# A large fused kernel on one core: the up weights of both expert stages made stationary, copied for each tile, with scaled result copies taken in turns

## Chip, cores and metric

The kernel runs on one core of one Trainium2 chip. The metric is the device time of one execution in microseconds (us), lower is better. A core has the engines TensorE (PE), VectorE (DVE), ScalarE (ACT), GpSimd (POOL) and SyncE (SP); each has an instruction queue of its own, and they meet through semaphores.

## What is computed

Two layers over a sequence of S = 4096 tokens of width D = 256, all float32. Layer 0 is x + SSD(xn) + MoE0(xn), layer 1 is x + attention(xn) + MoE1(xn), where xn is the layer norm of x. The change touches the two expert parts only:

```python
def _swiglu(x, w1, w3, w2):
    return jax.nn.silu(x @ w1.T) * (x @ w3.T) @ w2.T
# MoE0: 16 experts of width 128, 4 chosen for each token (grouped top-k of sigmoid scores)
# MoE1: 8 experts of width 512, 2 chosen for each token (softmax of the two top scores):
h1 = jnp.einsum('bsd,efd->bsef', x, W1)
h2 = jnp.einsum('bsd,efd->bsef', x, W2)
hidden = jax.nn.silu(h1) * h2
expert_out = jnp.einsum('bsef,edf->bsed', hidden, W3)
return jnp.einsum('bse,bsed->bsd', gating, expert_out)
```

The expert's result for a token is scaled by the token's gate weight and summed over its chosen experts.

## The kernel before

The program runs in stages: norm and routing of layer 0, the SSD stage (to about 1380 us), the first expert stage ("e0_", 1381 to 1631 us), the bridge (sum of the expert rows, layer norm, attention, routing of layer 1), and the second expert stage ("e1_", from 1910 us to the end). Both expert stages are the function expert_phase (from line 1218), with other sizes.

Routing has sorted the (token, expert) pairs into tiles of 128 rows, each tile of one expert: NT0 = 144 tiles in the first stage with f = 128, NT1 = 72 in the second with f = 512. A table etab in SBUF gives each tile's expert. All up weights (wup, 2f columns an expert) and down weights (wdown) of the stage lie in SBUF once SP has loaded them, expert after expert.

For each tile the kernel gathers its 128 token rows (xg), turns them on PE with two transposes (x_ps), copies them to SBUF (xgT, DVE), multiplies by the up weights (u_ps), takes silu of the first half (sil, ACT), multiplies sil, gate and the second half (hid, DVE), turns hid on PE with f/128 transposes (h_ps), copies that to SBUF (hidT, ACT), multiplies by the down weights (d_ps), copies the result (y, DVE), and POOL scatters the rows by an indirect DMA. In the first stage y goes to rows of its own; in the second it is added into the output in memory, one tile after another, each add waiting for the one before.

In the up matmul of before the stationary operand is xgT (128x128 of it, tokens as columns) and the moving one is the weights, read straight from wup at an address that depends on the expert: passes of 2f = 256 columns in the first stage, of 512 columns in two PSUM banks (UB = 2) in the second. u_ps has tokens as rows, and so hid has to be turned before the down matmul.

The order on every engine is the helper pipeline(nt, 3, step), which calls step once for each tile and three times more; in step s an engine works on tile s, s-1 (a), s-2 (b) and s-3 (c or d) as written out. On PE: x transposes of s (line 1394), up of s-1 (1405), the register load of the expert number of s (1386), hid transposes of s-2 (1416), down of s-3 (1424). On ACT: the DMA of a row tile eight tiles ahead (1331, first stage only), silu of s-1 (1343), hidT of s-2 (1348). On DVE: xgT of s (1359), in the first stage a piece of the Join work (1491 and 1497: 64 operations of 128x256 that sum x, SSD and shared rows, spread over tiles 54 to 139), hid of s-1 (1367), y of s-3 (1374). On POOL, first stage: target rows of s (1291), six bias adds of 128x1024 (1478, at tiles 50, 61, ... 105, each after a DMA of shared rows that SP issues in line 1455), scatter of s-3 (1308). On POOL, second stage: gather of s (1286), add of s-7 (1300). The rings: u_ps 2, sil, hid and hidT 2, y six tiles in the first stage and four in the second, d_ps two banks in the first stage and one in the second. SP loads the weights in lines 1213 and 1214.

Of the kernel before, what the change touches and what calls it, by code (L numbers as in the profile page):

```python
# [12 lines left out]
P = 128  # L13
# [1204 lines left out]
def expert_phase(nc, sem, tag, k, rows, lists, by_slot, etab, wup, wdown, e_n, f, nt, y_dram, load, s_first=None, beside=None):  # L1218
# [8 lines left out]
    with ctx:  # L1227
# [4 lines left out]
        AHEAD = 8  # L1232
# [4 lines left out]
        hid = sb("hid", [P, 2, f])  # L1237
        hidT = sb("hidT", [P, 2, f])
# [7 lines left out]
        h_ps = ps("h_ps")  # L1246
        d_ps = [ps("d0"), ps("d1")] if UB == 1 else [ps("d0")] * 2
        RD = 2 if UB == 1 else 1
# [3 lines left out]
        s_xt, s_xk, s_up, s_sil, s_hid, s_ht, s_hk, s_dn, s_yk = (sem(tag + n) for n in (  # L1252
            "x_turned", "x_kept", "up_done", "silu_done", "hidden", "hidden_turned", "hidden_kept",
            "down_done", "y_kept"))
        with nc.Block() as block:
# [25 lines left out]
            def _(pool):  # L1281
# [12 lines left out]
                def add_rows(n):  # L1294
                    pool.wait_ge(s_yk, n + 1)
# [8 lines left out]
                def scatter(n):  # L1304
                    pool.wait_ge(s_yk, n + 1)
# [21 lines left out]
            def _(act):  # L1327
                def next_rows(n):
                    act.wait_ge(s_hid, n - XR + 1)
                    act.wait_ge(s_target, n - XR + 1)  # L1330
                    act.dma_start(xg[:, n % XR, :], by_slot[n * P:(n + 1) * P, :]).then_inc(s_xg[n % XR], 16)
# [3 lines left out]

                def step(s):
                    if sorted_rows and XR <= s.n + AHEAD < nt:
                        next_rows(s.n + AHEAD)
# [5 lines left out]
                    b = s.back(2)  # L1344
                    if b.inside(nt):
                        reached(act, s_ht, b)
                        reached(act, s_dn, b, 2)
                        nc.scalar.activation(hidT[:, b.slot(2), :], h_ps[:, 0:f], ACT.Copy).then_inc(s_hk, 1)
# [3 lines left out]
            def _(dve):  # L1352
                v = nc.vector

                def step(s):
                    if s.inside(nt):
                        reached(dve, s_xt, s)
                        reached(dve, s_up, s, 2)
                        v.tensor_copy(xgT[:, s.slot(2)].rearrange("p c t -> p (c t)"), x_ps[:, 0:D]).then_inc(s_xk, 1)  # L1359
                    if beside:  # L1360
                        beside.tile(dve, s.n)
                    a = s.back(1)
                    if a.inside(nt):
                        reached(dve, s_sil, a)
                        reached(dve, s_ht, a, 2)
                        second = u_ps[a.slot(2)][UB - 1][:, f * (2 - UB):f * (3 - UB)] if UB == 1 else u_ps[a.slot(2)][1][:, 0:f]
# [13 lines left out]
            def _(pe):  # L1380
                held = {}

                def expert(s):

                    if s.n not in held:
                        held[s.n] = pe.value_load(etab[0:1, ds(s.n, 1)], min_val=0, max_val=e_n - 1)
                    return held[s.n]

                def step(s):
# [19 lines left out]
                    if s.inside(nt):  # L1409
# [746 lines left out]
```

## Time and profile before

| | |
|---|---|
| Median of three runs | 2352.23 us (2347.92 to 2357.65) |
| The profiled execution, its own time | 2354.6 us |
| Its span in the profile | 2352.9 us |
| Mean granted TensorE clock | 0.973 of full speed |
| PE busy, of the span | 2170.1 us, 92% |
| PE weight loads | 1588.1 us, 67% |
| DVE, ACT, POOL busy | 68%, 50%, 61% |
| DMA | 329 MB, 140 GB/s on average |

A page of the profile shows one execution. Busy times of an engine exclude register, branch, semaphore and DMA-issuing instructions. PE and PEld are TensorE's matmuls and its weight loads, which overlap. The ends of matmuls are modelled: a matmul record lasts longer than the distance to the next one. L1405 is line 1405 of the kernel. PEclk is the clock that was granted to TensorE, as a share of full speed.

### The profile page before, as it was taken

The page shows a single profiled execution, that of the slowest core. Times are in us where ns is not written, and L with a number is a line of the kernel's source. Part 1 is how long each engine was busy: PE and PEld are TensorE (multiplying, and loading weights), DVE is VectorE, ACT ScalarE, POOL GpSimd, SP SyncE. Part 2 cuts the span into 40 slices and gives each one's busy share as a digit, 9 for nine tenths or more (in the row PEclk, how much of TensorE's full clock was granted, in tenths as well). Part 3 has the DMA queues.
Part 4 walks back from the last instruction along what each step waited for, and adds up shares of the span by engine and source line. Part 5 has one row for each costly group of instructions (what it writes and reads, how often), then busy time and mean ns, then how long its engine had stood idle before and what let it go on. Part 6 is the DMA issues. An engine that isn't in the chain of part 4 may idle for free. (4 is left out here: it accounts for less than half of the span.)

```text
span 2352.9 us, 40732 instructions
## 1 busy us (share of the span) xinstructions
PE 2170.1 (92%) x12292; PEld 1588.1 (67%) x12292; DVE 1601.6 (68%) x3508; ACT 1186.1 (50%) x2671; POOL 1423.7 (61%) x1272
## 2 busy tenths in 40 slices
PE   4878999999999999999999989998698779999997
PEld 2446777777777777777777768786344656666665
DVE  5777888888888888888888856775878632222222
ACT  2456777777777777777777732222132431111111
POOL 1325777777777777777777757886635014444442
PEclk9998999999999999999999999999799889999999
DMA  9854444454454544555544548874520055222221
GB/s 322 320 134 129 140 140 140 138 157 137 146 152 143 144 135 147 146 153 144 149 140 135 144 129 250 271 249 158 208 95 1 1 203 150 45 45 43 44 45 19
DMA packets 193828, 329.02 MB, mean 140 GB/s; under 512 B 49236, under 2 KB 135509, under 8 KB 193365
## 3 DMA queue, kind: packets, MB, share of 16 engines
q1 hardware_dynamic: 137220, 232.12, 33.2%
q0 software_dynamic: 26880, 53.64, 8.8%
q10 hardware_dynamic: 29520, 40.66, 5.4%
q8 instruction: 110, 1.80, 0.3%
q14 instruction: 98, 0.79, 0.1%
HBM read 240.46 MB, written 86.79 MB: 139 GB/s over the span
## 5 line engine op out<-in xcount | busy, mean ns | idle before, releaser
L1014 DVE SCALAR_TENSOR_TENSOR m_cv<-m_hp,conv,m_cv 128x256 f32<-128x256 f32 x864 | 416.7, 482 | 112.1 <-ACT m_cv L913 90.9
L1405 PE MATMUL e_u<-wup,e_xgT 128*128 x1152 | 413.1, 492 | 0.5 <-DMA wdn<-in_w 0.5
L1343 ACT ACTIVATE e_sil<-e_u 128x128 f32<-128x128 f32 (+1 forms) x216 | 82.9, 384 | 525.2 <-PE e_u L1405 525.2
L840 POOL TENSOR_TENSOR m_er<-m_er,m_cT 128x1024 f32<-128x1024 f32 x128 | 301.7, 2357 | 45.8 <-DVE m_ar L1021 45.8
L951 ACT ACTIVATE m_ar<-m_ar,m_ta 128x128 f32<-128x128 f32 x1024 | 318.8, 390 | 0.8
L1102 PE MATMUL m_hp<-xnT,wpj 128*128 128x259 f32 x1152 | 304.7, 387 | 7.8 <-PEq L145 4.5
L1405 PEld LDWEIGHTS e_u<-wup,e_xgT 128*128 128x128 f32 x1152 | 205.2, 193 | 113.9 <-issue 105.9
L1110 PE MATMUL m_gp<-xnT,wpj 128*128 128x256 f32 x1024 | 268.7, 384 | 11.2 <-ACT m_gT L931 11.2
L1102 PEld LDWEIGHTS m_hp<-xnT,wpj 128*128 128x128 f32 x1152 | 214.1, 192 | 68.7 <-issue 27.4
L1300 POOL DMA_INDIRECT out<-e_y,target x72 | 113.0, 1569 | 229.2 <-DVE e_y L1374 199.3
L847 POOL TENSOR_TENSOR m_hdd<-m_hdt,m_tb 128x512 f32<-128x512 f32 x128 | 130.8, 1041 | 194.1 <-DVE m_hdt L1029 194.1
L1161 PE MATMUL m_out<-wo,m_gT 128*128 128x256 f32 x1024 | 242.9, 380 | 0.0
L931 ACT ACTIVATE m_gT<-m_gp,bias 128x256 f32<-128x256 f32 x256 | 121.1, 473 | 232.6 <-PE m_gp L1110 232.5
L1367 DVE SCALAR_TENSOR_TENSOR e_hid<-e_sil,gate,e_u 128x512 f32<-128x512 f32 x72 | 53.8, 747 | 255.2 <-ACT e_sil L1343 255.2
L1424 PE MATMUL e_d<-wdn,e_hidT 128*128 x864 | 224.3, 382 | 1.1 <-DVE e_y L1374 1.1
L1161 PEld LDWEIGHTS m_out<-wo,m_gT 128*128 128x128 f32 x1024 | 193.0, 190 | 47.7 <-issue 23.9
L1110 PEld LDWEIGHTS m_gp<-xnT,wpj 128*128 128x128 f32 x1024 | 178.6, 191 | 35.8 <-ACT m_gT L931 19.1
L881 POOL DMA_INDIRECT rows_by_slot<-m_xrow,posi x128 | 172.1, 1344 | 32.7 <-issue 28.2
L913 ACT ACTIVATE m_cv<-m_hp,m_bsum,conv 128x256 f32<-128x256 f32 x288 | 160.1, 556 | 56.9 <-PE m_hp L1102 55.3
L1308 POOL DMA_INDIRECT y_rows<-e_y,e_target x144 | 145.0, 1007 | 47.9 <-DVE e_y L1374 35.3
L1424 PEld LDWEIGHTS e_d<-wdn,e_hidT 128*128 128x128 f32 x864 | 147.3, 190 | 24.0 <-issue 2.1
L1047 DVE SCALAR_TENSOR_TENSOR m_y<-m_hT,dcol,m_yt 128x128 f32<-128x128 f32 x512 | 143.1, 342 | 23.7 <-PE m_yt L1150 23.7
(313 smaller groups left out, 3965.3 us busy)
## 6 DMA issues: line engine op xcount, KB each, us to landing
m_ar<-acum_rows_dram SPq DMA_DIRECT2D x512, 128.0 KB, 3.9
m_er<-eacum_rows_dram SPq DMA_DIRECT2D x128, 512.0 KB, 4.3
rows_by_slot<-blank_rows ACTq DMA_DIRECT2D x1, 18576.0 KB, 82.1
e_xg<-rows_by_slot ACTq DMA_DIRECT2D x132, 129.0 KB, 3.4
m_xrow<-xn_rows SPq DMA_DIRECT2D x32, 512.0 KB, 4.9
b_work<-y_rows SPq DMA_DIRECT2D x16, 1024.0 KB, 7.1
wup<-in_w SPq DMA_DIRECT2D x8, 1024.0 KB, 5.5
wpj<-in_w_proj SPq DMA_DIRECT2D x1, 4352.0 KB, 24.0
```

Source lines behind the costliest of these rows:

```text
L840: g.tensor_tensor(er[:, t], er[:, t], middle(cT[:, t * P:(t + 1) * P], HQ), ALU.mult).then_inc(scaled.sem, 1)
L881: pool.indirect_dma_start(by_slot, bass.IndirectOffsetOnAxis(posi[:, i * TB + t, r:r + 1], 0), xrow[:, t, r, :], None).then_inc(s_scat[t], 16)
L913: a(cv[:, n % 6, :], hp[n % 2][:, OLD:PW], ACT.Identity, bias=bsum[:, c:c + 1], scale=conv[:, c, OLD:TAPS]).then_inc(heva.sem, 1)
L951: ins = a(row, row, ACT.Exp, bias=ta[:, t, q * HQ + h:q * HQ + h + 1])
L1014: v_.scalar_tensor_tensor(o, hp[n % 2][:, j:j + BLK], conv[:, c, j:j + 1], o, ALU.mult, ALU.add).then_inc(tapped.sem, 1)
L1047: ins = v_.scalar_tensor_tensor(y1[:, cols], hT[:, conv_of(cc), t * P:(t + 1) * P], d_col[:, cc:cc + 1], yt[s % 2][:, cols], ALU.mult, ALU ...
L1102: ins = mm(hp[n % 2][:, 0:PW], w_proj[:, kd, col:col + P], xpad[:, kd, ds(i * BLK, PW)], start=kd == 0, stop=kd == KD - 1)
L1110: ins = mm(gp[:, 0:BLK], w_proj[:, kd, cc * P:(cc + 1) * P], xpad[:, kd, ds(i * BLK + OLD, BLK)], start=kd == 0, stop=kd == KD - 1)
L1161: ins = mm(out_ps[:, t * D:(t + 1) * D], gT[:, q % 2 * CQ + c, t * P:(t + 1) * P], w_out[:, cc, :], start=s == 0 and c == 0, stop=cc == CH ...
L1308: pool.indirect_dma_start(y_dram, bass.IndirectOffsetOnAxis(row_of(n), 0), y[:, n % YR, :], None).then_inc(s_y[n % YR], 16)
L1405: ins = nc.tensor.matmul(u_ps[a.slot(2)][b][:, 0:width], xgT[:, a.slot(2), c, :], wup[:, c, ds(e * (2 * f) + b * width, width)], start=c = ...
L1424: ins = nc.tensor.matmul(d_ps[d.slot(2)][:, 0:D], hidT[:, d.slot(2), c * P:(c + 1) * P], wdown[:, ds(e * (FC * D) + c * D, D)], start=c == ...
```

## The change

Both stages: the up weights become the stationary operand. Since the expert is only known at run time, ACT (and DVE for half of it in the second stage, halves = not sorted_rows) copies the tile's expert weights from wup into a ring of two, fixed, at fixed addresses; in the second stage that ring lies in the columns of xnT, which are free by then. The moving operand is xgT, 128 columns. The products come out with the hidden units as rows, as the down matmul wants them, so the hid transposes, h_ps and hidT go. With tokens as columns the gate can't be applied to hid any more, so it scales the result copy y: even tiles on ACT, odd tiles on DVE, each with a PSUM bank and a semaphore of its own. PE, ACT (and DVE in the second stage) each load the expert number into a register, a tile ahead. hid gets a ring of three, the row tiles are fetched seven ahead in place of eight.

```diff
-        AHEAD = 8
+        AHEAD = 7
-        hid = sb("hid", [P, 2, f])
-        hidT = sb("hidT", [P, 2, f])
+        hid = sb("hid", [P, 3, f])
+        halves = not sorted_rows
+        fixed = (xnT[:, :, 0:KD * 2 * f] if halves else sb("fixed", [P, 2, KD * 2 * f])[:]).rearrange("p r (c w) -> p r c w", c=KD)
-        h_ps = ps("h_ps")
-        d_ps = [ps("d0"), ps("d1")] if UB == 1 else [ps("d0")] * 2
-        RD = 2 if UB == 1 else 1
+        d_ps = [ps("d0"), ps("d1")]
+        s_yk = [sem(f"{tag}y_kept{n}") for n in range(2)]
+
+        def y_kept(eng, n):
+            if n >= 0:
+                eng.wait_ge(s_yk[n % 2], n // 2 + 1)
+
+        def reader(eng):
+            numbers = {}
+            def number(s):
+                if s.inside(nt) and s.n not in numbers:
+                    numbers[s.n] = eng.value_load(etab[0:1, ds(s.n, 1)], min_val=0, max_val=e_n - 1)
+                return numbers.get(s.n)
+            return number
...
             @block.scalar
                 def next_rows(n):
-                    act.wait_ge(s_hid, n - XR + 1)
+                    y_kept(act, n - XR)
...
+                number = reader(act)
                 def step(s):
+                    if s.inside(nt):
+                        e = number(s)
+                        act.wait_ge(s_w, e * 32 + 32)
+                        reached(act, s_up, s, 2)
+                        at = ds(e * (2 * f), 2 * f)
+                        if halves:
+                            nc.scalar.activation(fixed[:, s.slot(2), 0, :], wup[:, 0, at], ACT.Copy).then_inc(s_wa, 1)
+                        else:
+                            nc.scalar.activation(fixed[:, s.slot(2)], wup[:, :, at], ACT.Copy).then_inc(s_wa, 1)
                     if sorted_rows and XR <= s.n + AHEAD < nt:
                         next_rows(s.n + AHEAD)
                     a = s.back(1)
                     if a.inside(nt):
...
                         nc.scalar.activation(sil[:, a.slot(2), :], u_ps[a.slot(2)][0][:, 0:f], ACT.Silu).then_inc(s_sil, 1)
-                    b = s.back(2)
-                    if b.inside(nt):
-                        reached(act, s_ht, b)
-                        reached(act, s_dn, b, 2)
-                        nc.scalar.activation(hidT[:, b.slot(2), :], h_ps[:, 0:f], ACT.Copy).then_inc(s_hk, 1)
+                    number(s.back(-1))
+                    c = s.back(3)
+                    if c.inside(nt) and c.n % 2 == 0:
+                        reached(act, s_dn, c)
+                        landed(act, s_y, c, YR)
+                        nc.scalar.activation(y[:, c.slot(YR), :], d_ps[0][:, 0:D], ACT.Copy, scale=gate_of(c.n)).then_inc(s_yk[0], 1)
...
             @block.vector
+                    if halves and s.inside(nt):
+                        e = number(s)
+                        dve.wait_ge(s_w, e * 32 + 32)
+                        v.tensor_copy(fixed[:, s.slot(2), 1, :], wup[:, 1, ds(e * (2 * f), 2 * f)]).then_inc(s_wd, 1)
                     if beside:
                         beside.tile(dve, s.n)
...
-                        v.scalar_tensor_tensor(hid[:, a.slot(2), :], sil[:, a.slot(2), :],
-                                               gate_of(a.n), second,
-                                               ALU.mult, ALU.mult).then_inc(s_hid, 1)
+                        v.tensor_tensor(hid[:, a.slot(3), :], sil[:, a.slot(2), :], second, ALU.mult).then_inc(s_hid, 1)
+                    if halves:
+                        number(s.back(-1))
                     c = s.back(3)
-                    if c.inside(nt):
+                    if c.inside(nt) and c.n % 2:
                         reached(dve, s_dn, c)
                         landed(dve, s_y, c, YR)
-                        v.tensor_copy(y[:, c.slot(YR), :], d_ps[c.slot(2)][:, 0:D]).then_inc(s_yk, 1)
+                        v.tensor_scalar(y[:, c.slot(YR), :], d_ps[1][:, 0:D], gate_of(c.n), None, ALU.mult).then_inc(s_yk[1], 1)
...
             @block.tensor
                     a = s.back(1)
                     if a.inside(nt):
-                        e = expert(a)
-                        pe.wait_ge(s_w, e * 32 + 32)
+                        reached(pe, s_wa, a)
+                        if halves:
+                            reached(pe, s_wd, a)
                         reached(pe, s_xk, a)
                         reached(pe, s_hid, a, 2)
-                        for b in range(UB):
-                            width = 2 * f // UB
+                        for b in range(2 * FC):
+                            at = b * P % GT
                             for c in range(KD):
-                                ins = nc.tensor.matmul(u_ps[a.slot(2)][b][:, 0:width], xgT[:, a.slot(2), c, :],
-                                                       wup[:, c, ds(e * (2 * f) + b * width, width)],
+                                ins = nc.tensor.matmul(u_ps[a.slot(2)][b * P // GT][:, at:at + P],
+                                                       fixed[:, a.slot(2), c, b * P:(b + 1) * P], xgT[:, a.slot(2), c, :],
                                                        start=c == 0, stop=c == KD - 1)
                         ins.then_inc(s_up, 1)
-                    if s.inside(nt):
-                        expert(s)
-                    b = s.back(2)
-                    if b.inside(nt):
-                        reached(pe, s_hk, b, 1)
-                        reached(pe, s_hid, b)
-                        for c in range(FC):
-                            ins = nc.tensor.transpose(h_ps[:, c * P:(c + 1) * P], hid[:, b.slot(2), c * P:(c + 1) * P], k["ident"][:])
-                        ins.then_inc(s_ht, 1)
+                    number(s.back(2))
                     d = s.back(3)
                     if d.inside(nt):
-                        e = expert(d)
-                        reached(pe, s_hk, d)
-                        reached(pe, s_yk, d, RD)
+                        e = number(d)
+                        pe.wait_ge(s_w, e * 32 + 32)
+                        reached(pe, s_hid, d)
+                        y_kept(pe, d.n - 2)
                         for c in range(FC):
-                            ins = nc.tensor.matmul(d_ps[d.slot(2)][:, 0:D], hidT[:, d.slot(2), c * P:(c + 1) * P],
+                            ins = nc.tensor.matmul(d_ps[d.slot(2)][:, 0:D], hid[:, d.slot(3), c * P:(c + 1) * P],
                                                    wdown[:, ds(e * (FC * D) + c * D, D)], start=c == 0, stop=c == FC - 1)
```

POOL's two waits on s_yk (in add_rows and scatter) become y_kept as well.

## Rows read from the trace of the kernel before

In a timeline a row may stand for several operations in a stretch (x8), and [..] holds the idle time before it with what ended it.

**Rows 1.** Windows by stage: window, length, busy (count) by engine, clock, DMA, GB/s

```profile
1384.00:1630.00 246.00, 242.09 (x1296) 200.59 (x1294) 171.39 (x496) 64.59 (x289) 188.75 (x292) 0.98 0.75 234
...
1930.00:2336.00 406.00, 406.00 (x1535) 251.30 (x1534) 104.46 (x209) 75.97 (x140) 171.85 (x133) 1.00 0.32 63
```

**Rows 2.** Timeline, second stage, PE: start, us, engine, line, operation

```profile
2101.30 0.60 PE L1416 MATMUL e_h_ps<-ident,e_hid 128*128 128x128 f32 x4
...
2101.74 1.89 PE L1424 MATMUL e_d<-wdn,e_hidT 128*128 x8
...
2103.47 0.38 PE L1394 MATMUL e_x_ps<-ident,e_xg 128*128 128x128 f32 x2
...
2103.68 3.60 PE L1405 MATMUL e_u<-wup,e_xgT 128*128 x8
...
2109.29 0.38 PE L1394 MATMUL e_x_ps<-ident,e_xg 128*128 128x128 f32 x2
```

**Rows 3.** Timeline, first stage before the Join work

```profile
1408.69 0.38 PE L1394 MATMUL e_x_ps<-ident,e_xg 128*128 128x128 f32 x2
...
1408.91 1.03 PE L1405 MATMUL e_u<-wup,e_xgT 128*128 x4
...
1409.89 0.60 PE L1424 MATMUL e_d<-wdn,e_hidT 128*128 x2
1409.98 0.28 ACT L1343 ACTIVATE e_sil<-e_u 128x128 f32<-128x128 f32 x1 [1.18 <-PE e_u L1405]
...
1410.15 0.33 ACTq L1331 DMA_DIRECT2D e_xg<-rows_by_slot  x1
1410.15 0.27 ACT L1348 ACTIVATE e_hidT<-e_h_ps 128x128 f32<-128x128 f32 x1
...
1410.32 0.38 PE L1394 MATMUL e_x_ps<-ident,e_xg 128*128 128x128 f32 x2
```

**Rows 4.** Timeline, bridge (PE, PEld) and one row of the SSD stage

```profile
1855.77 1.95 PE L1746 MATMUL b_bank<-b_work 128*128 128x128 f32 x16
1857.55 1.04 PE L1737 MATMUL b_bank<-ident,b_work 128*128 128x128 f32 x8
...
1855.66 1.87 PEld L1746 LDWEIGHTS b_bank<-b_work 128*128 128x128 f32 x16
...
1348.84 0.85 PEld L1133 LDWEIGHTS m_yt<-m_er,m_state 128*64 128x64 f32 x16 [0.34 <-issue]
```

**Rows 5.** Groups by shape: busy us, mean ns of one, idle before

```profile
L939 ACT ACTIVATE m_sq<-m_gT 128x512 f32<-128x512 f32 x96 | 59.6, 621 | 14.4 <-DVE m_gT L1053 14.4
...
L619 ACT ACTIVATE small<-dt_z 128x1024 f32<-128x1024 f32 x1 | 1.1, 1057 | 0.0
...
L1064 DVE COPY m_cT<-m_hT 128x256 f32<-128x256 f32 x16 | 4.6, 286 | 2.0 <-ACT m_hT L924 2.0
...
L1348 ACT ACTIVATE e_hidT<-e_h_ps 128x512 f32<-128x512 f32 x72 | 42.6, 592 | 1.5 <-PE e_h_ps L1416 1.5
```

**Rows 6.** Source line 1386, the register load on PE: ns min/median/max

```profile
L1386 PEldq TENSOR_LOAD <-etab x216: 295/302/683, 1383.6 to 2322.9; - x108
L1386 PEldq FUSED_REGOPS  x216: 151/151/165, 1384.1 to 2323.3; - x108
```

**Rows 7.** Source lines 1291 and 1308, POOL, 1480 to 1560 us: ns min/median/max

```profile
L1291 POOL TENSOR_TENSOR e_target<-e_xg,e_slot_id x49: 195/205/488, 1480.5 to 1559.5; 128x1 int32<-128x1 int32 x49
...
L1308 POOL DMA_INDIRECT y_rows<-e_y,e_target x50: 968/982/1241, 1479.5 to 1559.9; - x50
```

**Rows 8.** Waits, 1480 to 1560, then 1560 to 1630: total, times, longest

```profile
POOL y_rows L1308 <- DVE e_y L1374: 1.3, 4, 0.9
...
POOL y_rows L1308 <- DVE e_y L1374: 8.5, 17, 1.7
```

**Rows 9.** Timeline, POOL at 1472; windows, 1480 to 1490

```profile
1472.58 2.35 POOL L1478 TENSOR_TENSOR j_sr<-j_sr,b_out_sb 128x1024 f32<-128x1024 f32 x1 [3.03 <-DMA j_sr<-shared_rows]
...
1480.00:1490.00 10.00, 8.12 (x35) 6.19 (x34) 5.95 (x18) 1.83 (x8) 8.17 (x14) 0.83 0.82 291
```

More of the change, by code:

```diff
@@ L1215, in expert_loads, with expert_phase @@
     return load
-def expert_phase(nc, sem, tag, k, rows, lists, by_slot, etab, wup, wdown, e_n, f, nt, y_dram, load, s_first=None, beside=None):
+def expert_phase(nc, sem, tag, k, rows, lists, by_slot, etab, wup, wdown, e_n, f, nt, y_dram, load, s_first=None, beside=None, xnT=None):
     ctx = ExitStack()
@@ L1251, in expert_phase @@
         s_y = [sem.lasting(f"{tag}y_scattered{n}") for n in range(YR)]
-        s_xt, s_xk, s_up, s_sil, s_hid, s_ht, s_hk, s_dn, s_yk = (sem(tag + n) for n in (
-            "x_turned", "x_kept", "up_done", "silu_done", "hidden", "hidden_turned", "hidden_kept",
-            "down_done", "y_kept"))
+        s_xt, s_xk, s_up, s_sil, s_hid, s_dn, s_wa, s_wd = (sem(tag + n) for n in (
+            "x_turned", "x_kept", "up_done", "silu_done", "hidden", "down_done", "up_fixed_by_scalar", "up_fixed_by_vector"))
+        s_yk = [sem(f"{tag}y_kept{n}") for n in range(2)]
[9 more added lines that the diff above has]
+            return number
         with nc.Block() as block:
@@ L1294, in add_rows @@
                 def add_rows(n):
-                    pool.wait_ge(s_yk, n + 1)
+                    y_kept(pool, n)
                     if n == 0:
@@ L1304, in scatter @@
                 def scatter(n):
-                    pool.wait_ge(s_yk, n + 1)
+                    y_kept(pool, n)
                     if sorted_rows:
@@ L1353, in _ @@
                 v = nc.vector
+                number = reader(dve)
                 def step(s):
@@ L1364, in step @@
                         reached(dve, s_sil, a)
-                        reached(dve, s_ht, a, 2)
-                        second = u_ps[a.slot(2)][UB - 1][:, f * (2 - UB):f * (3 - UB)] if UB == 1 else u_ps[a.slot(2)][1][:, 0:f]
-                        v.scalar_tensor_tensor(hid[:, a.slot(2), :], sil[:, a.slot(2), :],
-                                               gate_of(a.n), second,
-                                               ALU.mult, ALU.mult).then_inc(s_hid, 1)
+                        reached(dve, s_dn, a, 3)
+                        second = u_ps[a.slot(2)][UB - 1][:, f * (2 - UB):f * (3 - UB)]
+                        v.tensor_tensor(hid[:, a.slot(3), :], sil[:, a.slot(2), :], second, ALU.mult).then_inc(s_hid, 1)
+                    if halves:
+                        number(s.back(-1))
                     c = s.back(3)
-                    if c.inside(nt):
+                    if c.inside(nt) and c.n % 2:
                         reached(dve, s_dn, c)
                         landed(dve, s_y, c, YR)
-                        v.tensor_copy(y[:, c.slot(YR), :], d_ps[c.slot(2)][:, 0:D]).then_inc(s_yk, 1)
+                        v.tensor_scalar(y[:, c.slot(YR), :], d_ps[1][:, 0:D], gate_of(c.n), None, ALU.mult).then_inc(s_yk[1], 1)
                 if beside:
@@ L1380, in _ @@
             def _(pe):
[L1381 to L1387, printed above, removed]
+                number = reader(pe)
                 def step(s):
@@ L2111, in program @@
             with Semaphores(nc, sem) as own:
-                expert_phase(nc, own, "e1_", k, rows, lists1, None, etab1, wup, wdn, E1, F1, NT1, out, load, s_first=s_out)
+                expert_phase(nc, own, "e1_", k, rows, lists1, None, etab1, wup, wdn, E1, F1, NT1, out, load, s_first=s_out, xnT=xnT)
 def layout(i):
```

## The prediction

> **What bounds it now.** I read the windows by stage first. They are to be read for whether TensorE (PE) ever rests in the two expert stages: in the second one it is busy for all 406 of 406 us at a granted clock of 1.00, in the first for 242 of 246 [rows 1]. A busy PE need not be a full one, since the ends of matmuls are modelled, so the next view is the timeline of one tile, read for starts, not for durations. A record is one pass of a matmul; a matmul of these float32 operands has two passes, a transpose has one. In the second stage tiles follow each other by 5.82 us (2103.47 to 2109.29). By the starts the two x transposes are 0.21 of that, the eight up passes 3.44 (from 2103.68 to the hidden transposes at 2101.30 + 5.82; 0.43 each), the four transposes of the hidden rows 0.44 and the eight down passes 1.73 [rows 2]. They add up to the whole turn: this stage is the streaming of columns through PE, and nothing else. In the first stage the turn is 1.63 (1408.69 to 1410.32): 0.22 for x, 0.98 from the first up pass to the first down pass, 0.43 for down. A pass there costs 0.215 (four last 1.03, two 0.60, so two cost 0.43), which leaves 0.11 of the 0.98 to the one hidden transpose [rows 3]. There PE is not alone: GpSimd (POOL) becomes a second bound in its later part, below.
>
> **The change, second stage (72 tiles).** The four transposes go: -0.44. The up stage keeps its columns, but cuts eight passes of 512 into 32 of 128 columns, each with its own weight load. So the question is the pace of load and pass at 128 columns. The trace has it: in the bridge between the stages 16 passes of a full 128x128 stationary operand over 128 columns run from 1855.77 to the next group's start at 1857.55, which is 0.111 each, with 16 weight loads beside them [rows 4]. A quarter of 0.43 is 0.1075. So 32 x 0.111 = 3.56 in place of 3.44: +0.12. Net -0.32 a tile, x 72 = **-22.8 us**. The bounds of this term: at 0.1075, where the loads cost nothing, -31; where a load did not hide at all, each pass would take its 0.19 more (a load lasts 1.87 less 15 steps of 0.112 [rows 4]), 6.1 us a tile and some 400 us in all. I take 0.111 because those rows have the same shape, type and clock.
>
> The Trainium skill says otherwise (TensorE: Matmul & The Clock Gate, Back-to-back issue gap): in a stream of pairs of weight load and matmul it gives 81 ns for 128 columns and 131 ns for 512, so four narrow ones would cost 2.5 times a wide one. By that ratio 3.44 would become 8.5, and the stage 330 us longer. Rows 4 against rows 2 show 1.03 times, not 2.5, so the trace disagrees, for float32 at least.
>
> What comes in place of the transposes on the other engines is copies. ScalarE (ACT) copies 1024 columns from SBUF to SBUF: 1.06 by its nearest row [rows 5]. VectorE (DVE) copies the other half: the row of 256 columns is 0.29, so I estimate 0.6 to 1.1 for 1024. ACT loses the hidT copy of 0.59 and gains half of the scaled copies: 256 columns from PSUM lie between its rows of 128 (0.27) and 512 (0.59), say 0.4, halved 0.2. With silu 0.6 ACT comes to some 1.9 of a 5.5 us turn, DVE to some 2.5. The copy for tile s may start once up(s-2) is done, and is wanted a whole turn later. Cost: nothing, hidden by PE's 5.5; without that cover it would be the 1.06. The DVE copy could hold off POOL, which generates the gathers and adds; POOL is busy for 172 of 406 us there [rows 1], idle for 3.4 us a turn, so nothing again. The start is exposed: once the first weights have landed, the 1.06 of the copy now stands before the first up matmul, less the second tile's transposes and x copy that stood there before: +0.3 to +1. I take +0.3.
>
> **The change, first stage (144 tiles).** One transpose goes (-0.11), four up passes become eight (8 x 0.111 against 4 x 0.215: +0.03). Net -0.08 a tile, -12 us if PE alone set the pace. It does not:
>
> *POOL.* A turn on POOL is at best the target add 0.20 and the scatter 0.98: 1.2 and the gaps. But in the later part the adds take up to 0.49 and the scatters up to 1.24 [rows 7], and six bias adds of 2.35 [rows 9] come between, 0.2 a tile over 66 tiles. From 1479.5 to 1559.9 there are 50 scatters, 1.64 apart [rows 7], with next to no waiting for results, so POOL's turn is level with PE's 1.63. The waits say how much it can give [rows 8]: from 1480 to 1560 POOL waited for a result tile for 1.3 us in all, from 1560 to 1630 for 8.5. PE would gain 4 in the first of these stretches and 3.5 in the second, and the ring of six result tiles lets it run one or two tiles ahead. And what the first 50 tiles gain (50 x 0.08 = 4) is lost: POOL waits 3.03 us at 1472 for shared rows to land, by the SP queue's time and not by PE's [rows 9]. PE arrives earlier and waits longer; the clock of 0.83 after that stall stays. The first copy's 0.6 at the start of the stage is swallowed there too. Between 3 (the last stretch alone) and 12 (all of it) I take **-6 us**.
>
> *ACT.* This is the term no row shows. After silu it reads the expert number, makes the scaled copy every second tile, copies 512 columns, issues the row DMA, and waits for the next up. The prices: silu 0.28, register load 0.30 and its arithmetic 0.15, as on PE [rows 6], half of 0.4, copy 0.62 [rows 5], issue 0.33 [rows 3]. One after the other that is 1.9; but the issue runs beside the previous activation (both start at 1410.15 [rows 3]), and PE's register load runs beside its matmuls. If ACT's does too, its engine has 1.1 in a turn of 1.54. Bounds: 0, and +0.3 a tile. I take 0, as the DMA issue on ACT itself shows the overlap. Behind ACT's new wait for up(s-2) only work of the same turn is queued. DVE gets lighter here (half the result copies go).
>
> **Smaller edits.** Reading the number a tile ahead was so on PE already: nothing. Prefetching rows seven tiles ahead in place of eight: seven turns are still 10.8 us: nothing. Two result banks in the second stage: down never waited for one before the drain: nothing.
>
> **Sum.** -22.8 - 6 + 0.3 = -28.5. The profiled execution took 2354.6, so 2326.1 for it; it lies 2.4 above the median, 2352.2, which gives **2323.7 us**, 1.2% faster.
>
> **The rivals.**
> (a) Narrow passes stream freely (0.1075) and the first stage gives nearly everything: -31 - 12, 2309. For it: 16 loads of half width take 0.85 [rows 4], 0.053 each, so a whole one could follow by 0.107. Against: rows 4, and rows 8 for the first stage.
> (b) The first stage gives nothing, as POOL's later part or ACT takes PE's place (register load serial, DMA issue beside it: 0.28 + 0.45 + 0.2 + 0.62 + 0.1 = 1.65 against 1.63). Then 2352.2 - 22.5 + 3 at most: 2330 to 2333. For it: rows 8. Against: POOL's best turn of 1.2 and the gaps.
> (c) ACT becomes the bound of the first stage, its queue wholly serial: 1.9 to 2.0 a turn, +0.3 to +0.36 x 144 = +43 to +52, less 22.5: 2373 to 2381, **slower**. It decides from the turn that eats the second stage's gain: 1.63 + 22.5/144 = 1.79. For it: four kinds of queued work between two waits. Against: the overlap in rows 3. Half way, a turn of 1.75 to 1.8, is no change: about 2350.
> (d) The weight loads are what a pass costs, 0.19: the second stage +2.5 - 0.44 a tile, the first +0.66 - 0.11, together +150 and +80: about 2580. Rows 4 speak against it flatly. The Trainium skill's ratio for narrow passes, above, is this case in a stronger form.
> (e) That the change does not do what it says: PE would show hidden transposes still; the diff leaves none.
>
> The Trainium skill (SBUF — State Buffer, Who interferes with whom) says that a DVE copy within SBUF in a two-port mode shuts GpSimd out until it ends. Rows 7 agree in kind. In this change it would matter only in the second stage, where POOL has 3 us to spare.
>
> **How the numbers follow.** The forecast 0.58; (a) 0.10; (b) 0.16; half way of (c) 0.05; (c) itself 0.08; (d) 0.03. Faster by over 0.5% (about what a measurement of this kernel can tell from no change) is the first three: 0.84; same 0.05; slower 0.11. The forecast's own range is 2315 to 2330; with (a) and (b) it becomes 2309 to 2338, which leaves out the rest.
>
> **What would show it.** Second stage: a turn of 5.51 with 32 up records, PE busy all through, 0.111 a pass; a turn over 5.8 would break the main term. First stage: 1.54 from tile 3 to 50, then a longer wait of PE near 1475, then between 1.54 and 1.6. ACT idle before silu must stay above zero; if it is gone, and PE waits for the copied weights, (c) is right. If PE waits there for a result tile, it is POOL.

## The result, and the profile after

The change takes 2320.74 us at the median against 2350.22 for the kernel before: a ratio of 0.9877, 95% interval [0.9839, 0.9915]. That is over three executions (2319.22, 2320.74 and 2327.79 us); a fourth took 5334.84 us at a granted clock of 1.00, for a reason that no trace here shows, and is left out. Two further groups of runs of the same kernel gave 0.9872 [0.9853, 0.9891] and 0.9885 [0.9862, 0.9908]. The profiled execution took 2319.22, its span 2317.4.

Windows by stage of the kernel after. The first stage is over at 1615.7 here, the second runs to 2309:

```profile
1384.00:1630.00 246.00, 235.53 (x1737) 214.32 (x1737) 147.32 (x423) 151.84 (x362) 189.84 (x292) 0.97 0.75 242
1930.00:2309.00 379.00, 374.12 (x2833) 356.18 (x2831) 128.39 (x235) 122.75 (x168) 170.88 (x131) 1.00 0.31 57
1480.00:1490.00 10.00, 10.00 (x80) 9.38 (x79) 6.91 (x21) 6.53 (x16) 8.90 (x14) 1.00 0.95 313
...
1900.00:1910.00 10.00, 7.32 (x32) 6.55 (x33) 2.11 (x4) 3.29 (x3) 4.60 (x4) 0.51 0.75 270
```

Against [rows 1], ACT's work in the first stage has more than doubled (64.6 to 151.8 us) and DVE's has shrunk. The third row stands against the window of [rows 9]: the clock there was 0.83 and is 1.00, and PE no longer rests. The last one is the start of the second stage, of which more below.

Timeline of the kernel after, one tile of the second stage:

```profile
2096.45 0.38 PE L1419 MATMUL e_x_ps<-ident,e_xg 128*128 128x128 f32 x2
2096.65 0.47 ACT L1374 ACTIVATE e_y<-e_d,gate 128x256 f32<-128x256 f32 x1 [1.13 <-PE e_d L1443]
2096.67 3.74 PE L1431 MATMUL e_u<-e_xgT,xnT 128*128 128x128 f32 x32
...
2097.03 1.05 ACT L1359 ACTIVATE xnT<-wup 128x1024 f32 x1
2097.21 0.68 DVE L1390 COPY xnT<-wup 128x1024 f32 x1
2100.24 1.89 PE L1443 MATMUL e_d<-wdn,e_hid 128*128 x8
...
2101.97 0.38 PE L1419 MATMUL e_x_ps<-ident,e_xg 128*128 128x128 f32 x2
```

Read by the starts, as in [rows 2]: the turn is 2101.97 - 2096.45 = 5.52 (5.82 before), of which 0.22 are x, 3.57 the 32 up passes, 0.112 each, and 1.73 the down passes. The hidden transposes are gone. All turns from the fourth tile on are 5.52. The two copies of the weights (1.05 and 0.68) start when these passes have just begun and are done by 2098.1, four us before the next up passes want them (2102.19).

The same of the first stage, two tiles, against [rows 3]:

```profile
1407.77 0.38 PE L1419 MATMUL e_x_ps<-ident,e_xg 128*128 128x128 f32 x2
...
1408.16 0.47 ACT L1374 ACTIVATE e_y<-e_d,e_xg 128x256 f32<-128x256 f32 x1 [0.34 <-PE e_d L1443]
...
1408.68 0.63 ACT L1361 ACTIVATE e_fixed<-wup 128x512 f32 x1
1408.76 0.33 ACTq L1345 DMA_DIRECT2D e_xg<-rows_by_slot  x1
...
1409.22 0.26 ACT L1368 ACTIVATE e_sil<-e_u 128x128 f32<-128x128 f32 x1
1409.32 0.38 PE L1419 MATMUL e_x_ps<-ident,e_xg 128*128 128x128 f32 x2
...
1410.12 0.63 ACT L1361 ACTIVATE e_fixed<-wup 128x512 f32 x1 [0.65 <-DMA wdn<-in_w]
...
1410.93 0.38 PE L1419 MATMUL e_x_ps<-ident,e_xg 128*128 128x128 f32 x2
```

PE's turn is 1.55, then 1.61; over the first fifty tiles nearly all are 1.54 or 1.55 (1.63 before). ACT stands still for 0.65 us before its copy in the turn without a scaled copy. The profile puts that down to a weight transfer, but a register load lies there (it took 0.43 in this turn; source line 1266, ns min/median/max):

```profile
L1266 ACTq TENSOR_LOAD <-etab x216: 272/287/582, 1378.8 to 2288.2; - x108
L1266 ACTq FUSED_REGOPS  x216: 152/152/173, 1379.3 to 2288.5; - x108
```

**Where the 35.4 us between the two profiled executions went** (2354.6 against 2319.2), by the first and last records of each stage: 12.0 in the first expert stage (1383.6 to 1630.9 became 1380.4 to 1615.7), 19.6 in the second (435.7 became 416.1), 0.7 in the bridge, and 3.2 before either, in code that is the same and so is no gain. The medians differ by 29.5.

### The profile page after: what moved, and what is told of

It reads as the page before. It is cut to its first block and busy times, and to the rows that moved or that the text cites. A ratio compares the mean times of both kernels' runs of the same rounds, so it can differ in the third digit from the quotient of the medians.

```text
span 2317.4 us, 45270 instructions
## 1 busy us (share of the span) xinstructions
PE 2131.7 (92%) x14164; PEld 1717.9 (74%) x14164; DVE 1605.3 (69%) x3472; ACT 1326.4 (57%) x2779; POOL 1423.1 (61%) x1272
## 5 line engine op out<-in xcount | busy, mean ns | idle before, releaser
L1398 DVE TENSOR_TENSOR e_hid<-e_sil,e_u 128x128 f32<-128x128 f32 (+1 forms) x216 | 91.0, 421 | 302.9 <-ACT e_sil L1368 298.3
L1431 PE MATMUL e_u<-e_xgT,xnT 128*128 128x128 f32 x2304 | 271.9, 277 | 0.8 <-ACT xnT L1359 0.8
L1431 PEld LDWEIGHTS e_u<-e_xgT,xnT 128*128 128x128 f32 x2304 | 265.8, 194 | 1.2 <-ACT xnT L1359 1.1
L1102 PEld LDWEIGHTS m_hp<-xnT,wpj 128*128 128x128 f32 x1152 | 214.2, 192 | 68.8 <-issue 27.4
L1443 PE MATMUL e_d<-wdn,e_hid 128*128 x864 | 223.7, 382 | 0.6 <-DVE e_hid L1398 0.4
L1443 PEld LDWEIGHTS e_d<-wdn,e_hid 128*128 128x128 f32 x864 | 147.6, 191 | 13.6 <-issue 1.5
```

Of the source, the lines that this page charges most:

```text
L1102: ins = mm(hp[n % 2][:, 0:PW], w_proj[:, kd, col:col + P], xpad[:, kd, ds(i * BLK, PW)], start=kd == 0, stop=kd == KD - 1)
L1431: ins = nc.tensor.matmul(u_ps[a.slot(2)][b * P // GT][:, at:at + P], fixed[:, a.slot(2), c, b * P:(b + 1) * P], xgT[:, a.slot(2), c, :], s ...
L1443: ins = nc.tensor.matmul(d_ps[d.slot(2)][:, 0:D], hid[:, d.slot(3), c * P:(c + 1) * P], wdown[:, ds(e * (FC * D) + c * D, D)], start=c == ...
```

## The experiments

Stage times below run, for the first stage, from the first x transpose to the last one: 240.8 us before, 228.9 after.

**Each stage alone, and the change again.** A copy of the old expert_phase is kept, and one of the two calls uses it, here in e1_only; in e0_only it is the other call:

```diff
-                expert_phase(nc, own, "e0_", k, None, None, by_slot0, etab0, wup, wdn, E0, F0, NT0, y0, load,
+                expert_phase_old(nc, own, "e0_", k, None, None, by_slot0, etab0, wup, wdn, E0, F0, NT0, y0, load,
```

> The change in the second stage alone, the first stage as before. Theory (the gain there is four transposes of 0.11 less the dearer narrow passes, nothing else waits): the turn of the second stage is 5.52 us, the first stage's 1.63, and the kernel is 19 to 22 us faster than before, ratio about 0.991. Rival (the first stage gives the larger part, or the two stages' gains depend on each other): under 12 us, ratio over 0.995.

> The change in the first stage alone, the second as before. Theory A (the first stage gains its 0.08 us a tile over nearly all 144 tiles): 10 to 13 us faster, ratio about 0.995, turn 1.55. Theory B, that of the prediction (GpSimd and the wait for the shared rows take half of it): 6 us, ratio 0.9975, and a wait of the bias add for a DMA near tile 50. Rival (ScalarE's queue is serial): turn over 1.63, ratio 1.00 or more.

> The changed kernel once more, as a control on the same chip as the two halves. If the two halves add up, its gain is the sum of theirs, 29 to 35 us, ratio 0.985 to 0.988. The profile tells whether SP's chain of weight loads in the first stage again ends after some 69 us (before: 75) and whether the bias add near tile 50 again waits for nothing; if it waits 3 us or more this time, the missing wait was the luck of one execution.

Measured beside a kernel before of 2351.5: e1_only 2331.63, ratio 0.9913 [0.9896, 0.9931], 19.9 less; e0_only 2340.73, 0.9949 [0.9932, 0.9966], 10.8 less; the whole 2322.69, 28.8 less. The parts add up to 30.7, within the intervals. Turns were 5.52 and 1.55. The second stage gives a little less than forecast, the first nearly twice as much.

**Narrow passes alone.** The kernel before, its up pass cut into 128 columns, transposes and register addresses kept:

```diff
-                        for b in range(UB):
-                            width = 2 * f // UB
+                        for b in range(2 * FC):
+                            at = b * P % GT
...
-                                ins = nc.tensor.matmul(u_ps[a.slot(2)][b][:, 0:width], xgT[:, a.slot(2), c, :],
-                                                       wup[:, c, ds(e * (2 * f) + b * width, width)],
+                                ins = nc.tensor.matmul(u_ps[a.slot(2)][b * P // GT][:, at:at + P], xgT[:, a.slot(2), c, :],
+                                                       wup[:, c, ds(e * (2 * f) + b * P, P)],
```

> The kernel before with its up passes cut to 128 columns in both stages, transposes of hid, hidT and all else kept. Theory (a narrow pass with its load costs 0.111 to 0.112 against 0.1075 of a wide one's quarter): second stage's turn 5.82 + 32 x 0.112 - 3.44 = 5.96, first stage's 1.63 + 0.03 = 1.66, together +14 us, ratio 1.006. Rival (passes at 0.1075, loads cost nothing): no change. Rival (loads exposed): hundreds of us.

Measured: 2413.92, ratio 1.026 [1.0239, 1.0282]. The second stage did exactly what was expected: 5.96 a turn, so 32 narrow passes cost 0.14 more than 8 wide ones and the four transposes 0.44 (5.96 against the change's 5.52). This shows the main term by itself. The first stage did not: after a few turns of 1.65 to 1.77 they were mostly 1.85 to 2.5, 2.03 on average, where 1.66 was expected. Its timeline, PE, then source lines, of the first stage, of the second, and of the register load in the first:

```profile
1407.87 1.06 PE L1405 MATMUL e_u<-wup,e_xgT 128*128 x8
1409.29 0.30 PE L1416 MATMUL e_h_ps<-ident,e_hid 128*128 128x128 f32 x1 [0.36 <-issue]
...
1410.01 0.38 PE L1394 MATMUL e_x_ps<-ident,e_xg 128*128 128x128 f32 x2
...
1411.87 0.38 PE L1394 MATMUL e_x_ps<-ident,e_xg 128*128 128x128 f32 x2
```

```profile
L1405 PEldq FUSED_REGOPS  x576: 46/46/51, 1387.7 to 1678.6; - x192
```

```profile
L1405 PEldq FUSED_REGOPS  x1152: 46/46/46, 1970.1 to 2392.1; - x192
```

```profile
L1386 PEldq TENSOR_LOAD <-etab x144: 295/390/930, 1385.5 to 1676.8; - x144
```

The turn shown last is 1.86, and PE waits for "issue", for nothing but its own queue. That queue works out one address per moving operand that depends on the expert: 4 a tile in the first stage (2 in the kernel before) and 16 a tile in the second (4 before). The changed kernel has none on its up line, since the copies stand at fixed addresses. The trace gives the starts in PE's queue too. An address is 46 ns long, but from its start to the next one's are 0.124. All entries of a tile but the register load take 1.55 us in such a turn, and with a load of 0.307 that is 1.855, as between the loads at 1410.39 and 1412.24. The load itself lasted longer in this run, 0.434 at the mean where the kernel before has 0.313: 1.55 + 0.43 = 1.98, against turns of 2.03. So PE's own queue sets the turn there. In the second stage, where a turn has 5.96 us for it, the 16 addresses cost nothing. By the same reading the queue of the kernel before, with two addresses fewer, comes to 1.30 + 0.30 = 1.60 us of its turn of 1.63. This is an estimate, no run tests it, but it suggests that there was no room for more address work, and the copies at fixed addresses take it off PE altogether. Why the load lasted longer in this run is open.

**The copies taken away.** The changed kernel without ACT's and DVE's copies, PE loading always expert 0's weights:

```diff
-                            nc.scalar.activation(fixed[:, s.slot(2)], wup[:, :, at], ACT.Copy).then_inc(s_wa, 1)
...
-                                                       fixed[:, a.slot(2), c, b * P:(b + 1) * P], xgT[:, a.slot(2), c, :],
+                                                       wup[:, c, b * P:(b + 1) * P], xgT[:, a.slot(2), c, :],
```

> The changed kernel without the copies of the up weights: the up passes always load expert 0's weights at a fixed address, ACT's and DVE's copies and their reads of the expert number go, PE reads the number of its own tile. Leaves out: the choice of the expert's up weights (the output is another). Theory (the copies lie beside PE's passes and cost only where a stage starts, and a little of the first stage's later part): second stage still 5.52 a tile, first stage still 1.54 to 1.55 in its first 50 tiles, the start of the second stage 1 to 1.5 us sooner (the 7.87 between the first two up records falls to some 6.5), in all 0 to 5 us faster than the change. Rival (the copies hold PE up a little in every tile, by memory or by the wait): 0.05 or more off each turn, so 10 us or more faster than the change, with the first stage's turn at 1.50 or under or the second's at 5.47 or under.

Measured: 2351.47, ratio 0.9949 [0.9933, 0.9966] to a kernel before of 2363.5, 12 us over its usual. Timeline, PE, in the second stage and in the first:

```profile
2100.92 0.38 PE L1403 MATMUL e_x_ps<-ident,e_xg 128*128 128x128 f32 x2
...
2106.44 0.38 PE L1403 MATMUL e_x_ps<-ident,e_xg 128*128 128x128 f32 x2
```

```profile
1413.15 0.38 PE L1403 MATMUL e_x_ps<-ident,e_xg 128*128 128x128 f32 x2
...
1415.13 0.44 PE L1403 MATMUL e_x_ps<-ident,e_xg 128*128 128x128 f32 x2 [0.28 <-DVE e_xgT L1376]
...
1416.74 0.38 PE L1403 MATMUL e_x_ps<-ident,e_xg 128*128 128x128 f32 x2
...
1418.29 0.38 PE L1403 MATMUL e_x_ps<-ident,e_xg 128*128 128x128 f32 x2
...
1420.78 0.44 PE L1403 MATMUL e_x_ps<-ident,e_xg 128*128 128x128 f32 x2 [0.78 <-DVE e_xgT L1376]
```

In the second stage the turn is 5.52 as with the copies: they cost nothing there. From the second tile's x transposes to the third's (the "7.87 between the first two up records" of the expectation) are 5.63 us, and 7.93 in ahead8_new of the same batch: the copies cost 2.3 at the start, more than expected. Of these 0.98 are the first up pass's later start (1.46 after the second tile's transposes in place of 0.48), the rest is that its passes run slowly for longer. In the first stage the turns were irregular (1.98, 1.61, 1.55, 2.49), 262.8 us in all, with less work on ACT than the change has. That fits neither theory; the next runs deal with it. What the copies cost in a first stage with regular turns was not run.

**Rows fetched seven or eight tiles ahead**, in either kernel:

```diff
-        AHEAD = 8
+        AHEAD = 7
```

> The kernel before with one edit: rows fetched seven tiles ahead in place of eight. In the changed kernel the chain of weight transfers on the SP queue took 68.8 us (first stage; 69.4 and 68.3 in its relatives) where the kernel before took 74.9 and 72.7, and the bias add near tile 50 no longer waited for its shared rows (3.0 and 1.6 us before). Theory (fewer row transfers in flight leave the weight chain more of the DMA engines at its start): chain here 68 to 70 us, the wait at the bias add under 0.5 us, and the kernel 1 to 4 us faster than before. Rival (the chain is shorter for another reason, such as PE's different pace or fewer DVE copies): chain here 72 to 75, wait 1.5 to 3, time as before within 1.5 us.

> The changed kernel with one edit: rows fetched eight tiles ahead again. Theory (the distance sets the chain of weight transfers): chain 72 to 75 us, a wait of 1.5 to 3 us at the bias add near tile 50, and 1 to 4 us slower than the change. Rival (another part of the change shortened it): chain 68 to 70, wait under 0.5, time as the change within 1.5 us.

Measured in the same batch as no_copy, ten executions each: ahead7_old 2364.06, 1.0005 [0.9996, 1.0015]; ahead8_new 2359.8, 0.9987 [0.9978, 0.9997], its first stage 265.2 us with the irregular turns. The weight chain took 74.6 and 69.6 us. So did the distance cost 36 us? The version with eight was run again on another occasion, beside the change itself:

> The changed kernel itself, beside a second run of the one that fetches eight tiles ahead. In the batch with no_copy and no_bias the kernel before was 12 us slower than in the others, and both of these, which do less than the change, had irregular turns of 2.0 to 2.5 us in the first stage (some 260 us where the change took 229 from its first x transpose to its last). Theory (that is a state of that batch and the changed kernel would have had it too): here, where the kernel before takes its usual 2350, the change is 2320 to 2327 with a first stage of 229 to 231; if the kernel before takes 2360 or more here, the change has the irregular turns as well and takes 2345 to 2352. Rival (leaving work out on POOL or ACT itself breaks the rhythm of the first stage): the change is 26 us or more under the kernel before whatever that one takes.

> The changed kernel with rows fetched eight tiles ahead again, as in ahead8_new, beside the change on the same chip. ACT's fetch of row tile s+8 waits for the scaled copy of tile s-4, which the step before has only just made; with s+7 it waits for that of tile s-5. Theory (that wait stands in ACT's queue ahead of silu and costs a little in many turns): 8 to 14 us slower than after_third, the first stage's turns irregular at 1.6 to 2.4, ACT's silu late by its queue. Rival (the distance costs nothing, as the forecast has it, and ahead8_new was slow by the state of its batch): within 3 us of after_third, turns of 1.54 to 1.55.

Measured: after_third 2322.02, 0.9885 [0.9862, 0.9908]; ahead8_again 2323.06, 0.9898 [0.9876, 0.992], first stages of 228.5 and 229.8. The distance costs nothing, as forecast, and ahead8_new was slow by something in its batch: the same code took 36.7 us more there, 35.4 of them in the first stage. There the kernel before lost 12, and the changed form gained next to nothing over it. By stages its second one kept the gain (388.3 us from the first x transpose to the last, 406.7 in ahead7_old), but its first one took 13.6 more than that of ahead7_old (265.2 against 251.6, where the two forms have 229 and 241 otherwise). The old form lost its share after tile 60 and kept its first 50 turns of 1.63; the changed one has irregular turns from the seventh tile on. So the first stage's gain is not safe: in that batch it was a loss. It was the same chip in both batches. What it was stays open. The register loads and the DMA packets looked at kept their durations; what differs is when ACT goes on after PE's up passes. Waits from 1395 to 1455 us, the kernel after and no_bias (next section, same batch):

```profile
ACT e_sil L1368 <- PE e_u L1431: 0.4, 2, 0.2
```

```profile
ACT e_sil L1368 <- PE e_u L1431: 9.1, 9, 1.4
```

ACT's silu waited 2 times for 0.4 us in all in the one, and 9 times for 9.1 in the other, up to 1.4 at once. The changed kernel itself was not run in that batch; that it would have lost as much is inferred from ahead8_new.

On the weight chain neither theory held cleanly: 74.6 in the old kernel with seven, 69.6 and 71.8 in the new one with eight (the latter with a wait of 1.7 for shared rows), 68.1 to 69.4 in the new one with seven. So most of the shortening comes with the rest of the change, and by what is open. Longer turns shorten the chain as well: it took 65.3 in narrow_old, the old form with turns of 2.03, and 63.9 in two_loads below. That can't be the cause here, since the change's turns are shorter than those before.

**POOL relieved.** The changed kernel without the six bias adds:

```diff
-        self.nc.gpsimd.tensor_tensor(self.sr[:, g % 2], self.sr[:, g % 2], middle(self.b_out[:], BIG), ALU.add).then_inc(self.s_b, 1)
+        pool.sem_inc(self.s_b, 1)
```

> The changed kernel without POOL's six bias adds of 2.35 us in the first stage. Leaves out: the output bias of the first six groups of shared rows. Theory (POOL is what makes PE late in the first stage's later part: tiles 60 to 118 take 4.4 us more than at the turn of 1.54): this excess falls to 0.5 to 2 us and the stage, 235.3 us from its first x transpose to its last scatter, becomes 1 to 4 us shorter. Rival (ACT, with its number read and its copy, is what makes PE late there): excess still 3 to 5, stage 235 to 237.

Measured in one execution: 2346.59 in that batch, first stage 258.1 with irregular turns from the eighth tile on, long before the first bias add. It decides nothing.

**ACT loaded.** One more read of the expert number a tile, on ACT, in the first stage:

```diff
+                    if sorted_rows and s.inside(nt):
+                        act.value_load(etab[0:1, ds(s.n, 1)], min_val=0, max_val=e_n - 1)
```

> The changed kernel with one more read of the expert number per tile on ACT in the first stage, result unused; it should cost ACT 0.45 us a tile, between silu and the copy of the weights. Theory (ACT is behind PE's passes and has some 0.3 to 0.5 us of slack a turn): first stage's turn stays between 1.54 and 1.62, the kernel 0 to 12 us slower than the change. Rival (ACT's queue is already what sets the turn, or nearly): every turn grows by the 0.45 to about 2.0, +65 us, and PE waits for ACT's e_fixed in every tile.

Measured, one execution each: 2372.25 beside a kernel before of 2350.06 and y_on_dve, below, of 2319.77. The first stage took 277.4 us, 47.4 more than in y_on_dve: 0.33 a turn. Timeline, ACT:

```profile
1409.50 0.63 ACT L1361 ACTIVATE e_fixed<-wup 128x512 f32 x1 [1.24 <-PE e_u L1433]
...
1411.18 0.47 ACT L1376 ACTIVATE e_y<-e_d,e_xg 128x256 f32<-128x256 f32 x1 [0.89 <-issue]
...
1411.55 0.62 ACT L1361 ACTIVATE e_fixed<-wup 128x512 f32 x1
1412.07 0.27 ACT L1368 ACTIVATE e_sil<-e_u 128x128 f32<-128x128 f32 x1
1413.28 0.63 ACT L1361 ACTIVATE e_fixed<-wup 128x512 f32 x1 [0.94 <-issue]
```

and the waits from 1395 to 1455 us (total, times, longest):

```profile
ACT e_y L1376 <- issue: 13.9, 15, 1.2
...
PEld e_u L1433 <- ACT e_fixed L1361: 7.0, 17, 0.7
```

Each turn has 0.9 us in which ACT's engine stands still for nothing but its queue; with one load it is 0.5 in the kernel after. The load starts with silu and runs beside it, but the next activation comes only when the load and its arithmetic are through: a load more is 0.44 more. ACT's two turns here are 2.05 and 1.73 (by the starts of its copies). Less 0.44 each they would be 1.61 and 1.29, 1.45 on average: by this estimate the changed kernel's ACT has 0.1 us to spare in PE's 1.545. Of 0.44 more, 0.34 had to come out, and 0.33 did. The rival was nearer than the theory.

**Scaled copies all on DVE**, as before the change:

```diff
-                    if c.inside(nt) and c.n % 2:
+                    if c.inside(nt):
-                        v.tensor_scalar(y[:, c.slot(YR), :], d_ps[1][:, 0:D], gate_of(c.n), None, ALU.mult).then_inc(s_yk[1], 1)
+                        v.tensor_scalar(y[:, c.slot(YR), :], d_ps[c.slot(2)][:, 0:D], gate_of(c.n), None, ALU.mult).then_inc(s_yk[c.n % 2], 1)
```

> The changed kernel with all scaled copies of the result on DVE, as before the change, while the copies of the up weights stay where they are. Theory (the turns between ACT and DVE matter little, since DVE has room: it adds 0.24 us a tile there and takes it off ACT): first stage 233 to 239 us against 235.3, second stage's turn 5.52, in all within 3 us of the change. Rival (the turns are needed: with all of them DVE's copies and POOL's scatters, which slow each other, hold the first stage's later part): first stage 240 us or more, POOL waiting for DVE's result.

Measured, one execution: 2319.77 against 2350.06, the first stage 230.0, turns 1.54 to 1.55 and 5.52. The turns between the two engines bring nothing that can be seen. No version tried beats the change.

## Why the prediction was right, and where it was off

**The second stage, main term: right.** 5.51 forecast, 5.52 measured, with 0.112 a pass; e1_only shows it alone, and narrow_old its two parts alone. The copies lie wholly beside PE's passes (no_copy: the same 5.52). The rival in which narrow passes cost 2.5 times a wide one, from the Trainium skill (TensorE: Matmul & The Clock Gate, Back-to-back issue gap), is refuted for float32: narrow_old has 1.04 times.

**The start of the second stage: too cheap.** The step "I take +0.3" was off in size. Timeline of the kernel after:

```profile
1901.51 2.00 ACT L1359 ACTIVATE xnT<-wup 128x1024 f32 x2 [14.97 <-DMA wdn<-in_w]
...
1903.27 0.69 DVE L1390 COPY xnT<-wup 128x1024 f32 x1 [0.73 <-issue]
...
1904.06 6.58 PE L1431 MATMUL e_u<-e_xgT,xnT 128*128 128x128 f32 x32 [0.78 <-ACT xnT L1359]
```

ACT makes its first copy when the weights land, but DVE's stands behind the first x copy and its own register load (0.56 here, and 0.22 of arithmetic), so PE begins at 1904.06, 1.46 after the second tile's transposes, where the kernel before begins 0.48 after them: +0.98, the upper end of the forecast's own bounds. PE waits for DVE's copy there, which ends at 1903.96, although the row names ACT's. The first passes then run slowly: the 32 take 6.4 in place of 3.6, at a granted clock of 0.51 (the window from 1900 to 1910 above), which is the lower of its two levels, 1.2 GHz, after PE had stood still for 9.8 us. The kernel before has that as well (5.9 for its first eight passes in place of 3.44, 5.1 in e0_only), so only the difference is a cost of the change; the forecast had neither. From the second tile's x transposes to the third's are 7.88 us (7.27 in after_third, 7.93 in e1_only; in the old form 6.39 before and 5.60 in e0_only): +0.9 to +2.3. With 0.30 in place of 0.32 a turn this makes some -20 (19.6 between the profiled executions, 19.9 by e1_only) out of -22.5.

**The first stage: the sum too small, by a wrong step.** Forecast -6, measured -10.8 alone. The failing step is "what the first 50 tiles gain is lost: POOL waits for shared rows by the SP queue's time". It took SP's time as fixed. The chain of weight transfers (first to last of line 1213) took 74.9 us before and 68.8 after, the first shared rows were asked for at 1453.18 in place of 1462.45, and POOL's wait of 3.03 is gone (also in e0_only and after_third; 0.2 in after_again, 1.7 in y_on_dve). With it went the rest of PE that the forecast said would stay at clock 0.83: the excess over the regular turn in tiles 50 to 60 was 4.0 us before and 0.2 after. The profiled execution of before was a dear one in this: the same old stage in e1_only waited 1.65 and had an excess of 1.5. Why the chain is shorter is open, as said above. Of the 12.0 us between the two profiled first stages, 3.2 lie in the first fifty tiles, 4.6 in tiles 50 to 60, 2.0 in tiles 60 to 118 and 2.1 behind: the forecast had the first two at nothing.

**POOL as second bound: right.** Tiles 60 to 118 took 1.3 us more than at the regular turn before, 4.1 after (2.7 to 4.3 in its repeats and e0_only), so 2.7 of the 4.8 us that the shorter turn would bring there are lost. no_bias decides nothing on the cause, but the trace of the kernel after does. POOL's waits for a result from 1480 to 1560, against 9.2 and 0.6 us in the 60 us from 1395 to 1455:

```profile
POOL y_rows L1322 <- ACT e_y L1374: 0.2, 1, 0.2
```

In every tile from 50 to 116 the scatter starts some 1.1 us or more after the copy of its rows has ended (0.28 in the first 45 tiles), and the scatters follow each other by 1.64, as they did before. POOL is behind all that time, and its pace is what the stage has. It reaches PE by the ring of six result tiles:

```profile
ACT e_fixed L1361 <- issue: 12.7, 25, 0.7
...
ACT e_y L1374 <- DMA y_rows<-e_y,e_target: 3.9, 3, 2.0
```

ACT's scaled copy waits three times for an older scatter to land before its slot may be filled (DVE's copy did so once before, for 2.5). The first row is the register load of each turn; alone it does not make ACT the bound, as y_on_dve shows, where ACT has less to do and the stage takes the same. That DVE's copies are what makes POOL's adds and scatters longer there [rows 7] is not separated by any run.

**ACT: right number, wrong reason.** "If ACT's register load does too" run beside the activations, the forecast said, the engine has 1.1 in a turn of 1.54. It does so only for the 0.28 of silu; two_loads shows that the queue holds the next activation back, 0.44 for a load. The cost was 0 only because copy, silu, load and half a scaled copy come to some 1.45, with the DMA issue beside them. Rival (b) added the same work up, with a serial load, to 1.65: too much, since from its start to the next activation's a copy takes 0.52 and a scaled copy 0.37, less than their records of 0.63 and 0.47. So a bound by ACT was 0.1 us a turn away and not 0.4. Rival (c)'s price of 1.9 a turn is what two_loads has, by one load more than (c) counted.

**The smaller edits:** seven tiles in place of eight was priced at nothing, and ahead8_again is within 1 us. The scaled copies by turns cost and bring nothing that one execution shows.

**The sum.** -20 and -10.8 against -22.5 and -6: errors of 2.5 and 5 in opposite directions. Against the kernel before of the same runs the change was 26.6 to 29.5 less by the medians, where 28.5 was forecast. That the sum is this close is in part luck: the two errors cancel.

## What to carry to other kernels

With the float32 operands of this kernel a pass of 128 columns with its own weight load costs about a quarter of a pass of 512 (0.112 against 0.43 us), so the operand may be chosen by what it saves elsewhere (here a transpose and a copy for each tile). Where a queue is fixed in order, add up its entries by their starts, with register loads as serial; an engine that seems half idle by its busy share can be 0.1 us from being the bound, and a busy one can be held by its own queue. Where an engine never waits for its input over a long stretch, as POOL here, it is the bound there. And never take the time of a DMA chain on another queue as fixed when the stage around it changes.

## What was not expected of the hardware

- A register load holds ACT's next activation back: 0.29 and 0.15 us for the load and its arithmetic, beside the running activation at first and then seen as idle time of 0.5 before the next one, while a DMA issue of 0.33 in the same queue stands beside an activation.
- Addresses that depend on a register cost PE's queue: 46 ns long, 0.124 us from start to start, for each such moving operand. In narrow_old four of them and a register load fill the queue for 1.85 us where the passes need 1.66; in its second stage sixteen cost nothing in a turn of 5.96.
- The same code differed by 36.7 us between two batches of runs (ahead8_new and ahead8_again), nearly all in one stage with four engines in close step, while the stage that is PE alone kept its 5.52 to the hundredth.
